# Two one-column VectorE operations of a cross-attention and group-norm kernel, rewritten as tensor_scalar

## The reference, cut to what matters

```python
q = conv1x1(Wq, bq, y); k = conv1x1(Wk, bk, y); v = conv1x1(Wv, bv, x)
scores = einsum('bhdl,bhel->bhde', q, k) / sqrt(E)     # 8 heads, Dh = 16
attn = softmax(scores)
out = einsum('bhde,bhel->bhdl', attn, v)
o = conv1x1(Wo, bo, out) + x
mu, var = mean and variance of o over channels and positions
o_hat = (o - mu) * rsqrt(var + 1e-5) * gn_w + gn_b
```

## Time and profile before

| what | value |
|---|---|
| time, median of 3 runs | 171.17 us (169.48 to 171.58) |
| the profiled execution, its own time | 171.42 us |
| span of its records, first to last instruction | 169.3 us |
| mean granted TensorE clock | 0.982 |
| busy: PE, PEld, DVE, ACT, POOL | 157.6, 123.2, 150.8, 139.3, 97.7 us |

### The profile page before, as it was taken

One profiled execution on the slowest core, in us unless ns is written; L12 is line 12 of the kernel. 1 busy time (PEld: TensorE's weight loads), 2 busy tenths in 40 slices (PEclk: granted clock), 3 DMA queues, 4 the chain that ended last, 5 costly groups with the idle time before them and its releaser, 6 DMA issues. The chain is left out here.

```text
span 169.3 us, 3898 instructions
## 1 busy us (share of the span) xinstructions
PE 157.6 (93%) x934; PEld 123.2 (73%) x934; DVE 150.8 (89%) x684; ACT 139.3 (82%) x354; POOL 97.7 (58%) x162
## 2 busy tenths in 40 slices
PE   7898999999999999999999999999999999998720
PEld 7698777777888877777776878877777777885400
DVE  1655999999999999999999999999999999988761
ACT  3644679999999999999998989999999899977441
POOL 3014566666766667766666766677766666750110
PEclk9969999999999999999999999999999999999996
DMA  5997669989999999999999999999999987632333
GB/s 197 398 392 248 229 229 364 335 285 292 351 334 359 341 345 343 377 336 346 330 300 352 368 340 325 334 346 359 344 319 351 351 338 273 234 143 96 125 157 127
DMA packets 14278, 50.85 MB, mean 300 GB/s; under 512 B 1712, under 2 KB 1712, under 8 KB 14256
## 3 DMA queue, kind: packets, MB, share of 16 engines
q1 hardware_dynamic: 13824, 50.08, 82.9%
q10 hardware_dynamic: 432, 0.53, 0.9%
HBM read 33.82 MB, written 16.78 MB: 299 GB/s over the span
## 5 line engine op out<-in xcount | busy, mean ns | idle before, releaser
L606 PE MATMUL o_ps<-x_sb,m_sb 128*128 128x512 f32 x124 | 60.8, 613 | 0.0
L606 PE MATMUL g_ps<-hl_sb 128*128 128x258 f32 x256 | 47.5, 310 | 0.0
L429 DVE TENSOR_TENSOR hl_sb<-y_sb,hl_sb 128x512 fp32r<-128x512 f32 x64 | 43.7, 684 | 1.4 <-ACT hl_sb L316 1.0
L316 ACT CAST hl_sb<-y_sb 128x512 fp32r<-128x512 f32 x64 | 40.1, 630 | 1.9 <-DMA y_sb<-in_ctx_dram 1.9
L248 POOL TENSOR_TENSOR lsuma<-hl_sb 128x256 f32<-128x256 f32 x30 | 21.9, 730 | 33.0 <-DVE hl_sb L429 33.0
L515 DVE BATCH_NORM_STATS2 bn<-o_ps 128x6 f32<-128x512 f32 x62 | 40.1, 687 | 0.9 <-PE o_ps L606 0.9
L390 ACT ACTIVATE out_sb<-o_ps,shift,gain 128x1024 f32<-128x1024 f32 x31 | 37.5, 1210 | 0.1
L606 PEld LDWEIGHTS g_ps<-hl_sb 128*128 128x128 f32 x256 | 36.0, 196 | 0.2 <-DVE hl_sb L429 0.2
L606 PEld LDWEIGHTS o_ps<-x_sb,m_sb 128*128 128x128 f32 x124 | 21.2, 191 | 14.8 <-issue 14.8
L259 POOL TENSOR_TENSOR lsumb<-hl_sb 128x256 f32<-128x256 f32 x30 | 21.9, 732 | 14.5 <-DVE hl_sb L429 14.5
L289 POOL TENSOR_TENSOR rstd<-veps,nhalf 128x1 f32<-128x1 f32 x32 | 17.6, 549 | 12.0 <-DVE veps L563 12.0
(11 more groups left out here) (74 smaller groups left out, 293.2 us busy)
## 6 DMA issues: line engine op xcount, KB each, us to landing
y_sb<-in_ctx_dram SPq DMA_DIRECT2D x32, 512.0 KB, 6.1
x_sb<-in_x_dram SPq DMA_DIRECT2D x32, 512.0 KB, 7.1
out_dram<-out_sb SPq DMA_DIRECT2D x31, 512.0 KB, 6.2
w_in<-in_weights_dram ACTq DMA_DIRECT2D x1, 256.0 KB, 5.6
out_dram<-out_sb ACTq DMA_DIRECT2D x1, 256.0 KB, 2.7
out_dram<-out_sb SPq DMA_DIRECT2D x1, 256.0 KB, 2.8
cols<-in_columns_dram ACTq DMA_DIRECT2D x1, 3.0 KB, 3.4
```

The source lines that it names most:

```text
L316: nc.scalar.copy(hl_sb[:, b % SLOTS, chunks, 0:C], y_sb[:, b % SLOTS, chunks, :]).then_inc(h_ready, 1)
L429: nc.vector.tensor_tensor(hl_sb[:, b % SLOTS, chunks, C:2 * C], y_sb[:, b % SLOTS, chunks, :], hl_sb[:, b % SLOTS, chunks, 0:C].bitcast(F3 ...
L606: return nc.tensor.matmul(dst, lhsT, rhs, start=start, stop=stop, **more)
```

## The change

The same two results are computed from the same columns. The deviation becomes a tensor_scalar with mv as its one tensor and cp as a scalar column; the pivot becomes a tensor_scalar with colsum as its one tensor and two scalar columns (from x_sb and m_sb), in place of a scalar_tensor_tensor with two tensors and one scalar column. Waits, semaphores and order stay.

```diff
-                nc.vector.scalar_tensor_tensor(out=st_in[:, (b + 1) % 2, 2:3], in0=colsum[:, b % 2:b % 2 + 1],
-                                               scalar=x_sb[:, b % SLOTS, 0:1], in1=m_sb[:, b % 2, E:E + 1],
-                                               op0=ALU.mult, op1=ALU.add).then_inc(pivot_ready, 1)
+                nc.vector.tensor_scalar(st_in[:, (b + 1) % 2, 2:3], colsum[:, b % 2:b % 2 + 1], x_sb[:, b % SLOTS, 0:1],
+                                        m_sb[:, b % 2, E:E + 1], ALU.mult, ALU.add).then_inc(pivot_ready, 1)
...
-                nc.vector.tensor_tensor(st_in[:, b % 2, 0:1], mv[:, b % 2, 0:1], cp[:, b % 2:b % 2 + 1], ALU.add).then_inc(dev_ready, 1)
+                nc.vector.tensor_scalar(st_in[:, b % 2, 0:1], mv[:, b % 2, 0:1], cp[:, b % 2:b % 2 + 1], None, ALU.add).then_inc(dev_ready, 1)
```

## The result

The changed kernel takes 173.08 us (median of 6, 172.32 to 173.88) where the kernel before takes 170.48 (median of 6 beside it); the ratio is 1.0172, 95% interval 1.0128 to 1.0217. The forecast was 173.7 us (range 173.0 to 174.6), 1.5% more. In microseconds the kernel before measured 0.7 lower here than in the three runs that the forecast started from (170.48, not 171.17), so the measured difference is 2.60 us against 2.5 forecast, while 173.08 stands near the lower edge of the range. The profiled execution took 173.48 us, with a span of 171.5.

What follows compares the result with a forecast made beforehand. DVE's in-order queue was taken to bound the kernel: 2.65 us from longer instructions, less 0.35 for held records, plus 0.19 in the tail gives 2.49, say 2.5, on 171.17: 173.7 us, range 173.0 to 174.6.

Steps and rivals of the forecast that it cites:

- DVE's queue sets the turn: Between 20 and 150 us DVE's in-order queue sets the 4.57 us turn; longer DVE instructions lengthen it to 4.67.
- first rival: A scalar column costs nothing by itself: each turn 34 ns shorter, 1.0 us in all, total 169.8 us; chance 4%.
- The pivot's +45 ns: Pivot (L507) goes from 220 to 265 ns, the duration of L533 in the same form; range +40 to +60.
- The deviation's +48 ns: Deviation (L527) goes from 159 to 207 ns, taken between half-way 204 and L459's 210; bounds -17 to +106.
- 29 turns: Saturated stretch: 28 ordinary deviations at 48 ns and 29 pivots at 45 ns add 2.65 us.
- -0.35 for the held records: L507 at 16.73 and L527 at 99.09, ending with GpSimd instructions, are no longer held: -0.17 and -0.18 us.
- The tail, +0.19: After 150 us, three turns where the statistics product waits for DVE grow by 0.093, 0.045 and 0.048 us.
- L498 start 0.05 us late at 158.69: In the tail's second turn a matmul holds L498 0.05 us, covering the deviation; only 0.045 us counts.
- The reasoning on L533: L533, already one tensor and two scalar columns, lasts 265 ns; L507 starts a fixed time before its record's end.

Runs made afterwards that it cites:

- later512_before: The kernel before with a GpSimd memset of 128x512, changing no result, put ahead of L270 in each turn: 176.12 us, ratio 1.0342.
- square_stt: The kernel before with the square (L533) as two SBUF tensors and one scalar column, the form the pivot had: ratio 0.9985.
- later512_after: The changed kernel with a GpSimd memset of 128x512, changing no result, put ahead of L270 in each turn: 174.25 us, ratio 1.0241.
- the two veps kernels: The kernel before with one or both of L563's constants read from scalar columns set once: 170.62 us (ratio 1.0057) and 173.08 us (1.0191).
- later_before: The kernel before with a GpSimd memset of 128x256, changing no result, put ahead of L270 in each turn: ratio 0.9967.

## Why the prediction was right

The mechanism held; both prices were somewhat too small. The close match of the total is in part luck. By the traces the parts come to some 0.08 us less ahead of the first deviation, 2.72 more up to the 29th, 0.11 more in the turn behind it and 0.21 in the tail: 2.96 us, where the forecast had 2.49. The medians give 2.60, with an interval of 2.2 to 3.7 us (from the ratio) that takes in both.

- *DVE's queue sets the turn, and a longer record lengthens it in full.* Shown: no new wait, +53 ns behind each changed line, and each half alone gives its own share. What the prediction did not see is the other side. TensorE is 11 ns behind, so only a loss on DVE counts. Its first rival, 34 ns a turn shorter, could not have given 1.0 us: at most 29 x 0.011 = 0.3 us.
- *The pivot's +45 ns.* It was 54 in the record. The form was in the trace (L533, 265), but the same form with these columns takes 274.
- *The deviation's +48 ns.* It was 55, between the bounds, 4 ns above L459's 210. Both misses go one way: 93 ns a turn forecast, 106 found. Over 29 turns these 13 ns are 0.38 us, most of what the forecast lacks by the traces.
- *29 turns, -0.35 for the held records.* The +2.72 us in the middle are 28 x 0.106 = 2.97, less 0.25: the turn with the held deviation went from 4.80 to 4.69 us, and one at 131 us, where L429 starts late for a reason that the profile does not name, from 4.84 to 4.89 only. The hold itself was read rightly from two records, as later512_before and square_stt show. Of the first pivot's gain 0.16 were got, and 0.08 given back by L429, which the forecast had not followed.
- *The tail, +0.19.* Its first turn grew by 0.10 (4.112 to 4.213). The next was spoilt by the clock in the profile of after; in later512_after, which has the full clock there, it is 4.293 against 4.238, +0.055 for 0.045, and what lies behind the last deviation +0.05 for 0.048. (The prediction has L498 start 0.05 us late at 158.69. That is counted from the end of L527's record; by DVE's usual overlap it is 0.13 late. The deviation is covered either way.)
- *The reasoning on L533.* The start of L507 0.19 us behind L533 was put down to L533's length. It is the pivot's wait for L500. The sum was not hurt: the deviation stands ahead of L500 and shifts it too, and the pivot stands behind the wait.

## What to carry to other kernels

On a saturated VectorE, price an instruction of one column by its form: here 142 to 159 ns without a scalar column, 204 to 220 with one and 264 to 283 with two. Turning a second tensor into a scalar column is a loss of some 55 ns, unless GpSimd reads SBUF at that moment: then the two-tensor form is held to the end of GpSimd's instruction. Whether the exchange pays depends on how far that end lies behind the start: at 0.26 us it only drew level for the square (268 against 265 ns), at 0.36, for the deviation, the whole change won 1.9 us. Before a gain on an engine is hoped for, measure the turn of the next one by taking work away from the first.

## What the runs showed of the hardware

- A scalar column adds about 60 ns to a one-column tensor_scalar: 142, 204 and 264 ns with none, one and two (L563 and the two veps kernels). A second tensor in place of a scalar column is some 55 ns shorter (159 against 214, 220 against 274).
- A one-column DVE instruction with two SBUF tensors that starts inside a GpSimd tensor_tensor ends with it (383 and 432 ns in place of 159 and 220; a median of 377 in later512_before), if that end lies behind its own; with 0.14 us of it left the deviation kept its 159 (later_before). With one SBUF tensor and scalar columns it is not held (214 and 273 ns in the first two places, 214 in later512_after).
- A longer one is delayed less. L429 (two SBUF tensors, 512 columns) took 0.76 in place of 0.68 us with 0.23 us of L280 left at its start (changed kernel, 15.13 us), and 0.68 with 0.10 to 0.12 left (later512_after). It also takes 0.68 us beside L289 of GpSimd in each turn of the kernel before, though L289 runs 0.39 us into it.
- The clock of TensorE fell for some microseconds at the start or near the end in some executions of one kernel and not in others; in the last turn of the changed kernel that came to 0.79 us (5.085 against 4.293 at the full clock in later512_after), almost a third of what the change costs.
